# The second attention of a vision tower: strips through DRAM in halves, heads dealt out over more slots, class query ahead of the projection

## What is computed

```python
q, k, v = split(src @ in_proj_w.T + in_proj_b)            # 16 heads
scores  = einsum('bhqd,bhkd->bhqk', q, k) / sqrt(16)
ctx     = einsum('bhqk,bhkd->bhqd', softmax(scores), v)
dense   = ctx @ out_proj_w.T + out_proj_b
aw      = softmax((src @ Qp_w.T + Qp_b) @ (src @ Kp_w.T + Kp_b).T / 8)
# the 51 largest of each row of aw are kept and divided by their sum
sparse  = kept(aw) @ (src @ Vp_w.T + Vp_b)
x       = layernorm(src + sig * dense + (1 - sig) * sparse)
```

## Time and profile before

| | us |
|---|---|
| median of 3 runs | 1273.41 |
| lowest, highest | 1272.54, 1274.91 |
| the profiled execution | 1266.08 |
| its span, first to last instruction | 1264.3 |
| busy of the span: PE | 1014.5 (80%) |
| DVE | 765.5 (61%) |
| ACT | 382.2 (30%) |
| POOL | 467.4 (37%) |
| mean granted TensorE clock | 0.907 |

### The profile page before, as it was taken

One profiled execution on the slowest core, in us unless ns is written; L12 is line 12 of the kernel. 1 busy time (PEld: TensorE's weight loads), 2 busy tenths in 40 slices (PEclk: granted clock), 3 DMA queues, 4 the chain that ended last, 5 costly groups with the idle time before them and its releaser, 6 DMA issues. The chain is left out here.

```text
span 1264.3 us, 21795 instructions
## 1 busy us (share of the span) xinstructions
PE 1014.5 (80%) x6656; PEld 745.1 (59%) x6656; DVE 765.5 (61%) x1825; ACT 382.2 (30%) x943; POOL 467.4 (37%) x576
## 2 busy tenths in 40 slices
PE   0157989789999965379889789888779997788887
PEld 0155777486776743246556556555369996465555
DVE  7975666554222237367577667556507775688884
ACT  0242433112222221143344344343224442222221
POOL 4972010154000016123233224121136774476664
PEclk9978999759999996689889999898889998899999
DMA  9904500133111112553363463462040000000000
GB/s 316 340 2 142 192 0 1 34 111 116 59 59 60 62 39 64 83 110 105 61 129 94 71 127 91 58 129 92 24 160 1 0 0 1 1 9 17 8 17 18
DMA packets 66590, 94.85 MB, mean 75 GB/s; under 512 B 9176, under 2 KB 58792, under 8 KB 65232
## 3 DMA queue, kind: packets, MB, share of 16 engines
q1 hardware_dynamic: 63312, 85.48, 25.8%
q0 software_dynamic: 3200, 8.43, 2.2%
HBM read 53.28 MB, written 40.34 MB: 74 GB/s over the span
## 5 line engine op out<-in xcount | busy, mean ns | idle before, releaser
L2259 DVE TENSOR_REDUCE fa_nm<-fa_ps 128x2 f32<-128x514 f32 x128 | 82.9, 689 | 79.7 <-PE fa_ps L2503 79.1
L1505 PE MATMUL ex_ps<-we_raw,ex_xT 128*128 x320 | 117.7, 491 | 0.0
L2051 ACT ACTIVATE fa_eT<-fa_ps 128x512 f32<-128x512 f32 x128 | 72.5, 588 | 79.1 <-PE fa_ps L2568 77.3
L2503 PE MATMUL fa_ps<-fa_ks,fa_qs 126*128 126x258 f32 x256 | 65.8, 381 | 33.5 <-DMA fa_ks<-fa_qk_rows 19.3
L3308 PE MATMUL qf_ps<-qf_wg,qf_xT 128*128 128x352 f32 x272 | 90.1, 481 | 2.0 <-ACT qf_xT L3149 1.4
L451 PE MATMUL tk_ps<-tk_u,tk_qb 64*32 64x64 f32 x1024 | 23.9, 268 | 70.5 <-POOLq L318 56.7
L2568 PE MATMUL fa_ps<-fa_qs,fa_ks 128*128 128x256 f32 x256 | 66.0, 351 | 17.5 <-ACT fa_eT L2051 17.5
L1419 DVE COPY ex_hT<-ex_ps 128x384 f32<-128x384 f32 x40 | 22.3, 558 | 92.5 <-PE ex_ps L1514 92.4
L2503 PEld LDWEIGHTS fa_ps<-fa_ks,fa_qs 126*128 126x128 f32 x256 | 46.7, 240 | 49.5 <-issue 29.8
L3308 PEld LDWEIGHTS qf_ps<-qf_wg,qf_xT 128*128 128x128 f32 x272 | 50.7, 195 | 37.4 <-issue 6.8
L2939 PE MATMUL ff_ps<-ff_xT,wg_f 128*128 128x128 f32 x544 | 66.2, 282 | 3.2 <-ACT ff_xT L2838 3.2
(11 more groups left out here) (493 smaller groups left out, 2380.4 us busy)
## 6 DMA issues: line engine op xcount, KB each, us to landing
x_rows<-tk_zero SPq DMA_DIRECT2D x8, 2176.0 KB, 17.5
we_raw<-in_L_ffn_W SPq DMA_DIRECT2D x24, 384.0 KB, 8.1
fa_qs<-fa_qk_rows SPq DMA_DIRECT2D x16, 514.0 KB, 8.2
fa_ks<-fa_qk_rows SPq DMA_DIRECT2D x32, 257.0 KB, 10.4
ex_xin<-x_rows SPq DMA_DIRECT2D x40, 128.0 KB, 2.0
y_rows<-ex_y SPq DMA_DIRECT2D x40, 128.0 KB, 1.7
fa_rsb<-fa_rs_rows SPq DMA_DIRECT2D x32, 132.0 KB, 2.8
fa_qk_rows<-fa_qhl SPq DMA_DIRECT2D x32, 128.5 KB
```

The costliest lines, as they stand in the source:

```text
L1505: last = mm(ps[:, bank + t % 2, 0:HD], xT[:, t % 2, k, :], raw[:, ds(e, 1), m, k * HD:(k + 1) * HD], start=(k == 0), stop=(k == KC - 1))
L2051: cp(eT[:, j % 8, :], ps[:, ST + j % 2, :], ACT.Exp).then_inc(z["e_ready"], 1)
L2259: nc.vector.tensor_reduce(nm[:, :, j], ps[:, b:b + 2, 0:TOK], AX.X, ALU.max, negate=True).then_inc(z["max_done"], 1)
L2503: last = mm(ps[:, b + t, 0:WID], qs[0:TOPS, p, head(j, 1 + t * P, P)], ks[0:TOPS, p, head(j, 0, WID)], start=True, stop=True)
```

## The change

The strips go out and come back in two halves, heads 0 to 7 (chunk 0) and 8 to 15 (chunk 1). `q_out`, `k_out`, `q_in` and `k_in` become two semaphores each. PE projects q0, k0, q1, k1 in this order, and ACT, DVE and POOL work by chunk: twice as many instructions of half the length. The eight DMAs out are the same ones in another order, and all stand ahead of `max_rows(u, 1)`. The DMAs in become twelve of half the size: q0, k0, q1, k1. Head 0 waits for chunk 0, head 7 for chunk 1 (its slice of the keys reaches one column into it).

Heads go to slots 5 to 16, and their maxima to the slot behind on DVE. The round of slot 5 moves to slot 6, behind the maxima of heads 0 and 1. `class_query` moves from slot 8 to slot 5, ahead of `project`; `class_max` and `class_probs` move with it, and POOL does `class_blocks` ahead of `shared_context`. `sparse_scores` moves to slot 14 (DVE's `sparse_max` to 15), `values` to slots 16 and 17, behind all heads.

```diff
-    ROUNDS_AT = {0: 1, 1: 1, 3: 1, 4: 1, 5: 1, 7: 1, 8: 1}
+    ROUNDS_AT = {0: 1, 1: 1, 3: 1, 4: 1, 6: 1, 7: 1, 8: 1}
-    HEADS_AT = {10: (0, 1), 11: (2, 3), 12: (4, 5), 13: (6, 7), 14: (8, 9), 15: (10, 11), 16: (12, 13), 17: (14, 15)}
-    MAXES_AT = {11: (0, 1), 12: (2, 3), 13: (4, 5), 14: (6, 7), 15: (8, 9), 16: (10, 11), 17: (12, 13, 14, 15)}
+    HEADS_AT = {5: (0, 1), 6: (2,), 7: (3,), 8: (4, 5), 9: (6,), 10: (7,), 11: (8, 9), 12: (10,), 13: (11,), 14: (12,),
+                15: (13, 14), 16: (15,)}
...
             def body(u, p, more):
                 if more:
-                    strips_out(u + 1, 1 - p, 0, 0, "qh_ready", "q_out", "q_in")
-                    strips_out(u + 1, 1 - p, 0, 1, "ql_ready", "q_out", "q_in")
-                    strips_out(u + 1, 1 - p, 1, 0, "kh_ready", "k_out", "k_in")
+                    strips_of(u + 1, 1 - p)
                 max_rows(u, p, 1)
                 if more:
-                    strips_out(u + 1, 1 - p, 1, 1, "kl_ready", "k_out", "k_in")
-                    strips_in(u + 1, 1 - p, 0, "q_out", "q_in")
-                    strips_in(u + 1, 1 - p, 1, "k_out", "k_in")
+                    strips_back(u + 1, 1 - p)
...
+            def strips_back(u, p):
+                strips_in(u, p, 0, 0, "q_out0", "q_in0")
+                strips_in(u, p, 1, 0, "k_out0", "k_in0")
+                strips_in(u, p, 0, 1, "q_out1", "q_in1")
+                strips_in(u, p, 1, 1, "k_out1", "k_in1")
...
                 for sl in range(SLOTS):
-                    if sl == 1 and more:
-                        high_queries(u + 1, 1 - p)
-                    if sl == 2 and more:
-                        high_keys(u + 1)
+                    if more:
+                        for j in HEADS_AT.get(sl - 1, ()):
+                            head_max(u + 1, j)
+                            if j % 8 == 7:
+                                high_maxima(u + 1, j // 8)
+                    if sl in (1, 2) and more:
+                        high_queries(u + 1, 1 - p, sl - 1)
+                        high_keys(u + 1, sl - 1)
...
             def head_scores(u, p, j):
                 if j == 0:
-                    pe.wait_ge(z["q_in"], 32 * (u + 1))
-                    pe.wait_ge(z["k_in"], 64 * (u + 1))
+                    pe.wait_ge(z["q_in0"], 32 * (u + 1))
+                    pe.wait_ge(z["k_in0"], 64 * (u + 1))
...
+                if j == 7:
+                    pe.wait_ge(z["q_in1"], 32 * (u + 1))
+                    pe.wait_ge(z["k_in1"], 64 * (u + 1))
...
+                    if sl == 5 and more:
+                        class_query(u + 1)
                     if sl == 5 and not first:
                         project(u - 1, 1 - p)
-                    if sl == 8 and more:
-                        class_query(u + 1)
...
-                            if j == 9:
-                                sparse_scores(u + 1)
-                    if sl in (15, 17) and more:
-                        values(u + 1, 1 - p, (sl - 15) // 2)
+                    if sl == 14 and more:
+                        sparse_scores(u + 1)
+                    if sl in (16, 17) and more:
+                        values(u + 1, 1 - p, sl - 16)
```

More of the change, by code:

```diff
@@ L1689, in sparse_class_values, with strips_out @@
                 sp.dma_start(v2c[0:1, p, :], class_row(u)[:, SEQ:2 * SEQ]).then_inc(z["v2c_in"], 16)
-            def strips_out(u, p, part, a, ready, out, read):
-                sp.wait_ge(z[ready], u + 1)
+            def strips_out(u, p, part, a, c, ready, out, read):
+                sp.wait_ge(z[ready], 2 * u + c + 1)
                 if a == 0 and u >= 2:
@@ L1695, in strips_out, with strips_in @@
                 src, dst = (qhl, khl)[part], d["fa_qk"][part, p, a]
[L1696 to L1700, removed]
+                sp.dma_start(dst[:, 8 * c:8 * c + 8, :].rearrange("d h n -> h d n"), src[:, a, c, :]).then_inc(z[out], 16)
+            def strips_in(u, p, part, c, out, read):
+                sp.wait_ge(z[out], 32 * (u + 1))
                 if u >= 2:
@@ L2086, in body @@
                 if more:
-                    queries(u + 1, 1 - p)
-                    keys(u + 1)
+                    for c in range(KC):
+                        queries(u + 1, 1 - p, c)
+                        keys(u + 1, c)
                 probs(u, 1)
@@ L2136, in _ @@
             act.wait_ge(z["w_ready"], 1)
-            queries(0, 0)
-            keys(0)
+            for c in range(KC):
+                queries(0, 0, c)
+                keys(0, c)
             sparse_operands(0)
@@ L2376, in body @@
                         statistics(u - 1)
-                    if sl == 8 and more:
-                        class_max(u + 1)
-                    elif sl == 8:
-                        class_row_max()
-                    if more:
-                        for j in MAXES_AT.get(sl, ()):
-                            head_max(u + 1, j)
-                            if j % 8 == 7:
-                                high_maxima(u + 1, j // 8)
-                            if j in (13, 15):
-                                values(u + 1, 1 - p, (j - 13) // 2)
-                            if j == 9:
-                                sparse_max(u + 1)
+                    if sl == 15 and more:
+                        sparse_max(u + 1)
+                    if sl == 17 and more:
+                        values(u + 1, 1 - p, 0)
+                        values(u + 1, 1 - p, 1)
                     for _ in range(ROUNDS_AT.get(sl, 0)):
@@ L2398, in body @@
                 st.end()
-            high_queries(0, 0)
-            high_keys(0)
+            for c in range(KC):
+                high_queries(0, 0, c)
+                high_keys(0, c)
             mix_all(1)
@@ L2448, in turn_rows, with projected @@
                 last.then_inc(z["x_ps"], 1)
-            def projected(u, p, j, name):
+            def projected(u, p, j, c, name):
                 pe.wait_ge(z["x_taken"], u + 1)
-                if not isinstance(u, int) or u:
+                if c == 0 and (not isinstance(u, int) or u):
                     pe.wait_ge(z["max_done"], N * u + j - 1)
-                for c in range(KC):
-                    lo = (KC * j + c) * P
-                    for k in range(KC):
-                        last = mm(ps[:, SB + 2 * j + c, 0:TOK], w["qk"][:, k, lo:lo + P], xT[:, p, k, :],
-                                  start=(k == 0), stop=(k == KC - 1))
-                    last.then_inc(z[name], 1)
+                lo = (KC * j + c) * P
+                for k in range(KC):
+                    last = mm(ps[:, SB + 2 * j + c, 0:TOK], w["qk"][:, k, lo:lo + P], xT[:, p, k, :],
+                              start=(k == 0), stop=(k == KC - 1))
+                last.then_inc(z[name], 1)
             def sparse_operands(u, p):
@@ L2690, in _ @@
             turn_rows(0)
-            projected(0, 0, 0, "q_ps")
-            projected(0, 0, 1, "k_ps")
+            for c in range(KC):
+                projected(0, 0, 0, c, "q_ps")
+                projected(0, 0, 1, c, "k_ps")
             sparse_operands(0, 0)
```

102 lines of the change are left out of this document (56 added, 46 removed).

## The result

The changed kernel takes 1335.6 us (median; 1331.3 to 1339.4) where the kernel before takes 1274.2 beside it: ratio 1.048, 95% interval 1.044 to 1.052. It is slower, as forecast, but by 61 us and not by 30, and 1335.6 lies just above the range that ended at 1330. The profiled execution took 1339.4 us.

What follows compares the result with a forecast made beforehand. Strips' round trip plus heads was taken to set each body's period. First body +4.7, bodies 1 to 5 +26.8, body 6 +4.2, prologue -5.6: +30.1 on 1266.1, plus 7.3 for the median, say 1304 us; range 1272 to 1330.

Steps and rivals of the forecast that it cites:

- the step that was said to decide: DVE, head 0 to head 4's maximum: rounds and `keep_weights` among the maxima, 12.4 us in sum, hold head 6.
- the landing of chunk 0: Strip reads: the first half lands 21.2 us after the projection's start, half the bytes in half of 17.2 us.
- The prologue, -5.6: Before the first body: heads 0 to 6 done before chunk 1 lands, a gain of 5.6 us.
- Head 0 at T+21.2, bounds 19.9 to 24: PE in each body: head 0 starts 21.2 us after T, the projection's start, when chunk 0 lands; before, T+29.8.
- Head 0 to head 6, 12.5: PE in each body: head 6 waits for head 4's maximum and starts 12.5 us behind head 0.
- Head 6 to `sparse_scores`, 9.1 plus 2.3 for the clock: PE's quads, turned products, heads and transposes: 8.6 us plus 0.5 waiting on head 7's maximum; half clock adds 2.3.
- `sparse_scores` to the next projection, 8.2: End of each body: the stretch with both `values` takes 8.2 us, where it was 9.35.
- The clock, 2.3: PE around head 6: half clock for about six us costs 2.3 us per body, bounds 0 and 5.
- `max_rows(u, 1)` goes out a us later, and its reader ... runs behind head 0: nothing.: SP's row maxima of the second half: issued a us later, read by turned product 8 behind head 0, no cost.
- the clock costs nothing: Rival on PE's granted clock: bodies only 2.9 us or so longer, 16 us less in all, 1288; chance 0.18.
- Halves don't land early: Rival on strip reads: chunk 0 at T+24 gives 1324, at T+29.8 with chunk 1 1370; chance 0.14.
- Maxima keep up, and the kernel is faster: Rival on DVE: head 4's maximum within 8 us of head 0, bodies of 45.9 us, 1252; chance 0.15.

Runs made afterwards that it cites:

- e5: The changed kernel, nothing altered, on a chip of the second kind: 1305.4 us, ratio 1.031 to the kernel before.
- e11: The changed kernel with SP issuing the second half's row maxima and chunk 0's reads ahead of chunk 1's writes: 1307.1 us, ratio 1.022 to the kernel before.
- e1: The changed kernel with the last three rounds and `keep_weights` moved ahead of the maxima of heads 0 and 1: 1252.8 us, ratio 0.993 to the kernel before.
- e9: The changed kernel, nothing altered, on a chip of the first kind: 1341.8 us, ratio 1.048 to the kernel before.
- e15: The changed kernel with POOL's gathers moved behind the low maxima of heads 8 to 15, first kind: 1317.2 us, ratio 1.035 to the kernel before.
- e3: The changed kernel with PE repeating head 5's product 14 times, on a chip of the second kind: 1288.5 us, ratio 1.020 to the kernel before.
- e10: The changed kernel with PE repeating head 5's product 14 times, on a chip of the first kind: 1317.9 us, ratio 1.033 to the kernel before.
- e12: The kernel before with halves, class query ahead, three rounds at once, heads from slot 9, on the first kind: 1266.0 us, ratio 0.992 to the kernel before.
- e13: The kernel before, nothing altered, traced on a chip of the first kind: 1265.4 us in its one profiled execution.

## Why the prediction was right and wrong

The sign held, and so did the step that was said to decide: rounds between the maxima hold head 6 back. Two steps failed. One is a term, the landing of chunk 0, put too early by 1.5 (e5) to 2.1 us (first trace) in the mean of bodies 1 to 5. The other is an encounter that the sum put at nothing without a word: on chips of the first kind POOL's gathers, released earlier, run beside quad 3 and delay its release.

On a chip like the one whose trace it was worked out from, the forecast came nearer: the span of e5's profiled execution is 37.7 us longer than before's, against a forecast sum of 30.1, and the medians on that chip are 41 us apart. That e5's 1305.4 stands beside the forecast 1304 is in part luck: the sum added 7.3 us for the median of the kernel before, which on that chip (1264.1) lies below the traced 1266.1.

- **The prologue, -5.6.** Measured -4.9 (e5) and -5.1: right.
- **Head 0 at T+21.2, bounds 19.9 to 24.** T+21.9 to 23.4 in e5, mean 22.7, and 23.3 in the changed kernel's first trace. The means are inside the bounds (one body, at T+24.02, is just outside) but 1.5 and 2.1 us late; with the first body, forecast at T+19.3 and measured at T+22.9 and T+20.9, that makes 11 to 12 us in bodies 0 to 5. The failed step is "I take reads to flow from T+12.6 ... Chunk 0 is half of their bytes ... so it lands at 12.6 + 17.2/2": from their first issue at T+12.2 it took 10.6 us to head 0 in e5, with chunk 1's traffic ahead and behind, and 8.7 or less with that held back (e11). The idle time ahead of head 0, put at 2.6 us, is 2.8 to 4.3 in e5.
- **Head 0 to head 6, 12.5.** Measured 12.3 to 12.7 in bodies 1 to 5 of e5. This was the step that decides, and e1 shows it by removing it.
- **Head 6 to `sparse_scores`, 9.1 plus 2.3 for the clock.** 10.2 to 12.0 in bodies 1 to 5 of e5.
- **`sparse_scores` to the next projection, 8.2.** 8.3 to 8.4 in bodies 1 to 5 of e5; 11.7 to 13.9 in the four bodies of the first trace with a late release of 2.5 us or more.
- **The clock, 2.3.** Of the right size, but the upper bound, "a second fall in the thin tail", is what happens in the bodies with a late release: there `values` takes up to 3.8 us for 1.98. The range took its two upper bounds one at a time, for 1324 and 1323; both together, by its own numbers, are 1343, and on chips of the first kind both were neared at once.
- **"`max_rows(u, 1)` goes out a us later, and its reader ... runs behind head 0: nothing."** Nothing was seen of it.

What the sum lacked altogether is the encounter of quad 3 with POOL's gathers. The prediction asked which work of SP and DVE the heads are moved past, but not what POOL does when its wait on the maxima ends earlier: the maxima of heads 0 to 7 release `low_maxima` and, behind it, four gathers. In the first trace this is four late releases of some 2.6 us and one of 1.1, with the clock at its lower level behind the four. Bodies 0 to 5 exceed the forecast by 25.7 us: the stretch behind `sparse_scores`, where the release is awaited, by 17, head 0 by 12, while the other stretches stay 4 under it. In e5, without late releases, they exceed it by 8.5: head 0 by 11, the stretch behind `sparse_scores` by 1, the others 3 under. On chips of the first kind taking the encounter away gives 1.3 points (e9 to e15, two chips). The 15.7 us of the experts' stage lie in both kernels on such chips, and no step could have had them from a trace in which they are absent.

Of the rivals, "the clock costs nothing" is refuted by e3 and e10. "Halves don't land early" is refuted by every trace in its far half (T+29.8); its near half (T+24) is where head 0 nearly was, T+23.3 in the first trace. "Maxima keep up, and the kernel is faster" describes what e1 makes of the change in sign and mechanism. That its 1252 stands beside e1's 1252.8 is luck: it meant 21 us less than 1273 and bodies of 45.9 us, and e1 is 10 us below the 1262.6 of its chip, with bodies 1 to 5 of 47.5.

## What to carry to other kernels

When work on an in-order engine moves ahead of a wait, count what the wait now holds back. Here three rounds that cost nothing in the strips' flight cost 6.6 us in each body behind head 0, and one line that put them back in front turned a 3% loss into a 0.7% gain on chips of the second kind (it was not tried on the first). When a wait ends earlier, follow everything that its semaphore releases on every engine, asynchronous work included, and see what it will run beside. And a trace of before and one of after may come from chips that differ: compare a stage that the change doesn't touch before the difference is put down to the change.

## What the runs showed of the hardware

- On three of five chips, when a block of contexts (34 short instructions on PE) runs beside POOL's indirect DMAs, its release reaches ACT and DVE up to 2.8 us late. Mostly it comes 1.8 to 2.1 us behind the start of the fourth and last of these DMAs; in e12, where the block starts 0.4 us behind the first of them, it comes 3.1 us behind the block's start and ahead of the fourth. On two chips the same overlap costs nothing (e5: quad 3 at 740.27, copy at 741.38, gathers issued from 738.22 to 742.13). In e13 other products beside the gathers show no "remote". Why the block of contexts, and why these chips, is open.
- The same chips lose 13 to 16 us in the routed experts' stage, where POOL also issues indirect DMAs. That this is the same effect was not tried.
- Products that compute nothing, put where PE would idle, paid for themselves: 28 instead of 2 for one head of each body (4.1 us) made the kernel 14 to 24 us faster through the granted clock.
